# Two graph layers on one core: the twelve main matmuls of a unit issued over two PSUM banks in turn

## The reference

```python
def _L0_gnn_ref(h, adj, W_neigh, b_neigh, W_self, b_self):
    deg = jnp.sum(adj, axis=1, keepdims=True) + 1e-05
    h_neigh = (adj / deg) @ h
    out = h_neigh @ W_neigh.T + b_neigh + h @ W_self.T + b_self
    return jax.nn.relu(out)

def _L1_gnn_ref(x, adj, W, b):
    rowsum = adj.sum(axis=1)
    d = jnp.where(rowsum > 0, rowsum ** (-0.5), 0.0)
    support = (d[:, None] * adj * d[None, :]) @ x
    return jax.nn.relu(support @ W + b)

x = _layernorm(x + _L0_gnn_ref(x, adj, ...), axis=-1)
x = _layernorm(x + _L1_gnn_ref(x, adj, ...), axis=-1)
```

## Time and profile before

| what | value |
|---|---|
| median of 3 runs | 800.5 us (799.44 to 802.32) |
| profiled execution, first to last instruction | 800.8 us |
| its own time beside that span | none is given; the span is 0.3 us over the median |
| PE busy | 782.1 us of 800.8, 3704 matmuls |
| PE weight loads busy | 653.0 us, 3704 loads |
| DVE busy | 577.4 us |
| ACT busy | 386.9 us |
| DMA | 160.93 MB, mean 201 GB/s |
| mean granted TensorE clock | 0.995 of full speed |

### The profile page before, as it was taken

How to read it: one execution, slowest core, us unless ns; L and a number is a source line. 1 busy time by engine, 2 the same in 40 slices (tenths; PEclk the granted TensorE clock), 3 DMA queues, 4 the chain that set the end, 5 groups by cost and what they waited for, 6 DMA issues and landing times.

```text
span 800.8 us, 11034 instructions
## 1 busy us (share of the span) xinstructions
PE 782.1 (98%) x3704; PEld 653.0 (82%) x3704; DVE 577.4 (72%) x868; ACT 386.9 (48%) x528; POOL 0.3 (0%) x6
## 2 busy tenths in 40 slices
PE   7899999999999999999999999999999999999995
PEld 4678888888888888888888888888888888888884
DVE  5799989899898998989966554555546455554643
ACT  3463745536446364454554545445444544545451
POOL 0000000000000000000000000000000000000000
PEclk9999999999999999999999999999999999999998
DMA  8767574755647556465565575746575574657540
GB/s 258 274 252 239 179 244 154 253 183 166 236 155 236 193 174 236 157 233 189 181 227 165 175 255 174 250 162 237 180 236 187 171 246 162 236 180 239 180 158 27
DMA packets 54459, 160.93 MB, mean 201 GB/s; under 512 B 5024, under 2 KB 18464, under 8 KB 54432
## 3 DMA queue, kind: packets, MB, share of 16 engines
q1 hardware_dynamic: 46224, 152.46, 56.6%
q10 hardware_dynamic: 8208, 8.13, 2.9%
HBM read 152.17 MB, written 8.39 MB: 201 GB/s over the span
## 4 chain that ended last, share of the span: by engine, by line
PE 94%; DMA 2%; DVE 2%; ACT 1%; issue 0%; SPq 0%
PE ps_main L675 84%; PE ps_epi L613 8%; DMA raw<-adj_t 2%; PE ps_main L657 1%; PE ps_epi L634 1%; DMA tt<-x_nat 1%; DVE lo L389 0%; DVE acc L565 0%; ACT hi L256 0%; PE ps_epi L693 0%; DVE tt L436 0%; DVE stats L585 0%; DVE tt L419 0%; DVE xs L389 0%; ACT tt L359 0%
## 5 line engine op out<-in xcount | busy, mean ns | idle before, releaser
L256 ACT ACTIVATE hi<-raw 128x1024 fp32r<-128x1024 f32 x254 | 269.4, 1061 | 352.8 <-PE ps_main L675 327.8
L389 DVE TENSOR_TENSOR lo<-raw,hi 128x1024 fp32r<-128x1024 f32 x254 | 310.4, 1222 | 145.3 <-ACT hi L256 145.2
L675 PE MATMUL ps_main<-hi,xs 128*128 128x512 f32 x1136 | 366.3, 392 | 4.3 <-DVE lo L389 4.3
L675 PE MATMUL ps_main<-hi,zs 128*128 128x512 f32 x896 | 283.0, 390 | 0.0
L675 PEld LDWEIGHTS ps_main<-hi,xs 128*128 128x128 f32 x1136 | 214.2, 189 | 49.3 <-DVE lo L389 3.6
L675 PE MATMUL ps_main<-lo,xs 128*128 128x512 f32 x568 | 222.4, 392 | 0.0
L675 PEld LDWEIGHTS ps_main<-hi,zs 128*128 128x128 f32 x896 | 168.3, 188 | 34.3
L675 PE MATMUL ps_main<-lo,zs 128*128 128x512 f32 x448 | 174.7, 390 | 0.0
L565 DVE TENSOR_TENSOR acc<-acc,raw 128x1024 f32<-128x1024 f32 x112 | 136.3, 1217 | 0.0
L675 PEld LDWEIGHTS ps_main<-lo,xs 128*128 128x128 f32 x568 | 107.3, 189 | 20.0 <-issue 0.2
L675 PEld LDWEIGHTS ps_main<-lo,zs 128*128 128x128 f32 x448 | 84.2, 188 | 16.3
(11 more groups left out here) (74 smaller groups left out, 322.7 us busy)
## 6 DMA issues: line engine op xcount, KB each, us to landing
raw<-adj_t SPq DMA_DIRECT2D x256, 512.0 KB, 3.3
res<-x_nat SPq DMA_DIRECT2D x11, 512.0 KB, 6.4
xt_sb<-xt SPq DMA_DIRECT2D x8, 512.0 KB, 5.0
x_scratch<-tt ACTq DMA_DIRECT2D x8, 512.0 KB, 6.2
res<-x_scratch SPq DMA_DIRECT2D x8, 512.0 KB, 6.0
out<-tt ACTq DMA_DIRECT2D x7, 512.0 KB, 6.4
tt<-x_nat SPq DMA_DIRECT2D x4, 512.0 KB, 6.4
acc<-x_nat SPq DMA_DIRECT2D x2, 256.0 KB, 3.6
```

Of the source, the lines that this page charges most:

```text
L256: return act.activation(dst, src, ACT.Copy)
L389: return dve.tensor_tensor(dst, src, hi_part.bitcast(f32), ALU.subtract)
L675: last = pe.matmul(ps[:, f, :], stationary(layer, part, jt, f), mov[:, slot(u), cols], start=(jt == 0 and i == 0), stop=(jt == JT - 1 and ...
```

## The change

The loops of a unit are nested otherwise. Before: half f outermost, then tile q, then the three passes, so that six matmuls in a row go to one bank. After: tile q outermost, then the three passes, then half f, so that each pass is a pair of matmuls with the same moving operand, the first into the bank of half 0 and the second into that of half 1. The twelve matmuls are the same twelve, and each bank gets its six in the same order as before. In the last unit `half_done` is raised after the last matmul of each half, which is now the eleventh and the twelfth of the unit.

```diff
                     ends = layer == 1 and is_last(b) and u == NU - 1
-                    for f, q in [(f, q) for f in range(FH) for q in range(UJ)]:
+                    for q in range(UJ):
                         jt = u * UJ + q
                         cols = slice(q * IB, (q + 1) * IB)
                         for i, (part, mov) in enumerate(((0, hi), (0, lo), (1, hi))):
-                            last = pe.matmul(ps[:, f, :], stationary(layer, part, jt, f), mov[:, slot(u), cols],
-                                             start=(jt == 0 and i == 0), stop=(jt == JT - 1 and i == 2))
-                        if ends and q == UJ - 1:
-                            last.then_inc(half_done, 1)
+                            for f in range(FH):
+                                last = pe.matmul(ps[:, f, :], stationary(layer, part, jt, f), mov[:, slot(u), cols],
+                                                 start=(jt == 0 and i == 0), stop=(jt == JT - 1 and i == 2))
+                                if ends and q == UJ - 1 and i == 2:
+                                    last.then_inc(half_done, 1)
```

## The result

The changed kernel takes 802.36 us in the median of 19 runs (801.18 to 804.52), the kernel before 800.87 us in as many (799.44 to 802.69). The ratio is 1.0018, with a 95% interval of 1.0010 to 1.0026: the change costs 0.8 to 2.1 us. That is slower by a little, and under the 0.3% that the prediction took as the smallest telling difference.

A forecast was written before the change was run, and what follows sets the result against it. PE was taken as the bound: the distance between main matmul starts times 3048, then the serial end over ACT, DVE and PE. 800.8 + 0.0 (main matmuls) + 0.0 (waits) + 1.1 (end) = 801.9 us profiled, median 801.6, range 799.0 to 804.3.

The forecast's parts named there:

- limit of 0.3%: Whole kernel time: a difference under 0.3% (2.4 us) can't be told from none.
- its starting point: Time of the kernel before, 800.5 us as the median of 3 runs, to which the predicted change was added.
- range of 5.3 us: Whole kernel time, 799.0 to 804.3 us: 801.6 with 2.7 either way for the undecided start behind products.
- The main distance: Between starts of the 3048 main matmuls, 0.2267 us each: the new order changes it by 0.000 us per matmul.
- reserve of 13 ns: Main matmuls: 0.0133 us of each distance is not columns, judged from half clock; up to 41 us in all.
- the faster rival: Main matmuls: pairs shorten the distance by all or half of 0.0133 us, giving 761 or 781 us; 8 in 100.
- The end: Last unit: half 0 is signalled after the eleventh matmul, not the sixth, so the whole end moves by +1.13 us.
- Half 1 was covered: Program end: DVE finishes half 1 at 790.53, PE needs it near 791.4, so it is covered by 0.8 us.
- The slow starts: First five distances behind each of 92 products: 0.03 us extra per unit, left unchanged, bounds -2.8 to +2.8 us.
- The two rivals on the clock: PE's idle end halves its clock, 803.0 us, 4 in 100; bank cycling costs main-stream clock, e.g. 863 us, 2 in 100.

The follow-up runs named there:

- The third experiment: Units 1 to 14 of each block change bank at every matmul, neighbours sharing no moving operand, against the kernel before; one run, 802.19 us.
- the fourth: From the second block on, main matmuls share one stationary piece and, per unit, the same moving columns; base kernel not named; one run, 800.74 us.
- the bf16 kernels: Kernel before and changed kernel, each with split parts in bf16 instead of fp32r: 760.2 us (ratio 0.9502) and 761.34 us (0.9517 to before).

## Why the prediction was right

It said no measurable change, 801.6 us, +1.1 us from the end of the program; measured were +1.5 us of medians with an interval of 0.8 to 2.1. So a change was measured, in the direction and about of the size that the prediction had put in its sum. It could be told from none because there were 19 runs of each kernel; the prediction's limit of 0.3% was drawn from three. Of the 0.8 us between 801.6 and 802.36, 0.4 are its starting point, 800.5 from three runs where 19 gave 800.87. Its range of 5.3 us would have held a loss of nothing as well, so it is the rows of the end, not the time, that put it to the test.

*The main distance, 0.000 us.* Right. Its three arguments (a change of bank seen once per unit, the same pair seen 256 columns wide, loads that are issued and timed alike when they repeat) all pointed the same way, and the stretches of 744.68 us on both sides confirm them together. The third experiment and the fourth confirm them apart: banks in turn without a shared operand, and shared operands throughout. The reserve of 13 ns, which made the faster rival thinkable, was read from the half clock; the bf16 kernels show that 11 of it can be had, but by the type and not by the order.

*The end, +1.13 us.* Right to the hundredth: 4.07 instead of 2.94, ACT 0.43 us after the eleventh matmul (787.12 to 787.55), PE's idle time 1.19. That the last unit is where the price arises was shown by taking it out (2.94 us again, ratio 1.0001) and by making it alone (4.07 us, ratio 1.0017). Half 1 was covered as said: DVE was done at 788.18 + 1.29 = 789.47, and PE's thirteenth small matmul, 1.54 us after 788.92, needed it at 790.46: covered by 1.0 us, where the prediction had 0.8.

*The slow starts.* Left as they are with bounds of 2.8 us to either side; they stayed as they are. That was a default, not an argument: the prediction said that it did not know what sets them, and it is still not known. With these bounds the range was wider than needed.

*The two rivals on the clock.* The prediction read the line of the clock as full in all but the last slice; it overlooked that a 9 can hide the half clock of its own, which both kernels have ahead of 32 us. Neither rival came all the same: the clock was 1.00 from 32 to 787 us, where PE now changes bank at every matmul, and again from 788 to 791 us, so the 1.19 us of idle time at the end did not stretch the small matmuls: their first 15 take 2.08 us from 788.92 to 791.00 in the chain, against 2.06 before:

```profile
788.92 2.08 PE ps_epi L694 x15
```

By what is told of cycling through banks (the Trainium skill, TensorE: Matmul & The Clock Gate, A second HAM failure mode: psum-queue depth-cycling), of a bf16 kernel whose matmul groups had small idle times between them, this kernel was a candidate for a swinging clock. Here the clock stayed at its upper level, and PE waited nowhere between 42.67 us and the end of the last unit.

*What is left of +1.5.* 0.36 us more than the end explains. It lies within the interval, and no stretch of the trace shows it; the start of the program, whose length varies by 2.1 us from trace to trace, can hide it. The two parts taken apart (1.0001 and 1.0017) point at no second cause, but their intervals are too wide to exclude one of that size in the start.

## What to carry to other kernels

A reordering of matmuls that changes neither their number nor what their engine waits for is priced by the distance between their starts, and the trace of before may hold the new neighbourhood already, as it did here, once per unit and in a smaller shape. Its cost may sit where a result is handed on: interleaving two accumulations finishes both at the end, where finishing one first lets the next engines start on it. Keep the interleaved order, if at all, away from the last unit ahead of a serial tail.

## What the runs showed of the hardware that I had not expected

- The distance of 512-wide matmuls on fp32r, 226.7 ns, was the same with six in a row to a bank and with banks in turn, and with other and with the same moving and stationary operand; on bf16 it is 215.8 ns. The loads take 188 and 98 ns.
- The first five distances after a row of smaller matmuls take 1.16 instead of 1.13 us on fp32r, whether two or six small ones went ahead. On bf16 they take 1.08, as any five do.
- A type of two bytes for the split parts gave 5% (ratio 0.9502) in a kernel that is bound by PE, while the order of its matmuls gave nothing.
